# Another order of the attention work items in a fused attention and mixture-of-experts kernel on one core

## The reference

```python
q = _rope((x @ wq_w.T + wq_b).reshape(b, t, NH, HD).transpose(0, 2, 1, 3))
k = _rope((x @ wk_w.T + wk_b).reshape(b, t, NKV, HD).transpose(0, 2, 1, 3))
v = (x @ wv_w.T + wv_b).reshape(b, t, NKV, HD).transpose(0, 2, 1, 3)
k, v = jnp.repeat(k, G, axis=1), jnp.repeat(v, G, axis=1)
att = jnp.einsum('bhqd,bhkd->bhqk', q, k) / HD ** 0.5
att = softmax(where(causal, att, -inf))
y = jnp.einsum('bhqk,bhkd->bhqd', att, v)
x = layernorm(x + y.transpose(0, 2, 1, 3).reshape(b, t, c) @ cp_w.T + cp_b)
# then: x = layernorm(x + shared expert(x) + the four routed experts of each token(x))
```

## Time and profile before

| | |
|---|---|
| time, median of 3 runs | 551.11 us |
| span of the profiled execution | 548.3 us |
| PE busy | 525.8 us, 96% |
| DVE busy | 435.9 us, 79% |
| ACT busy | 372.3 us, 68% |
| POOL busy | 290.6 us, 53% |
| chain that ended last | PE 75%, DVE 10%, POOL 6% |
| granted TensorE clock, mean | 0.998 |

### The profile page before, as it was taken

One profiled execution on the slowest core, in us unless ns is written; L12 is line 12 of the kernel. 1 busy time (PEld: TensorE's weight loads), 2 busy tenths in 40 slices (PEclk: granted clock), 3 DMA queues, 4 the chain that ended last, 5 costly groups with the idle time before them and its releaser, 6 DMA issues.

```text
span 548.3 us, 12215 instructions
## 1 busy us (share of the span) xinstructions
PE 525.8 (96%) x3796; PEld 359.4 (66%) x3796; DVE 435.9 (79%) x1126; ACT 372.3 (68%) x841; POOL 290.6 (53%) x336
## 2 busy tenths in 40 slices
PE   8999999999999899989999898899999999999885
PEld 4656444444554454534433387799999999999874
DVE  2388989899889899999992177987878788787685
ACT  2444777787888688968879566366766667667534
POOL 5121232555412777267978856477644454545292
PEclk9999999999999999999999999999999999999999
DMA  5934174400523811321042352378544443341495
GB/s 150 179 66 65 31 191 145 82 8 21 91 62 88 207 58 46 82 81 51 32 128 82 104 178 66 112 227 262 159 139 128 130 118 111 111 133 46 160 414 194
DMA packets 53710, 64.96 MB, mean 118 GB/s; under 512 B 8091, under 2 KB 47406, under 8 KB 53648
## 3 DMA queue, kind: packets, MB, share of 16 engines
q1 hardware_dynamic: 45968, 46.45, 31.4%
q0 software_dynamic: 7056, 17.60, 9.2%
q10 hardware_dynamic: 624, 0.13, 0.1%
HBM read 32.49 MB, written 25.62 MB: 106 GB/s over the span
## 4 chain that ended last, share of the span: by engine, by line
PE 75%; DVE 10%; POOL 6%; issue 3%; ACT 2%; DMA 2%; SPq 1%; POOLq 0%; DVEq 0%; ACTq 0%
PE psH L1705 13%; PE psS L1506 12%; PE psO L1491 11%; PE psT L1476 10%; PE psS L1568 4%; PE psX L1673 3%; PE psG L1716 3%; PE psS L1511 2%; PE psS L1592 2%; POOL xs_scratch L766 2%; PE psY L1733 2%; PE psY L1730 2%; PE psY L1729 2%; PE psY L1732 2%; PE psY L1731 2%
## 5 line engine op out<-in xcount | busy, mean ns | idle before, releaser
L885 ACT ACTIVATE prob<-psT 128x512 f32<-128x512 f32 (+3 forms) x384 | 167.3, 495 | 51.6 <-PE psT L1476 49.0
L1161 DVE TENSOR_REDUCE MX<-psS 128x1 f32<-128x512 f32 (+3 forms) x344 | 182.6, 595 | 9.1 <-PE psS L1511 3.9
L1506 PE MATMUL psS<-KS,QS 96*128 96x512 bf16 (+3 forms) x384 | 109.9, 328 | 4.4 <-DVE MX L1161 2.5
L839 POOL DMA_INDIRECT y_scratch<-ys,dst x79 | 76.9, 973 | 65.7 <-ACT ys L1040 50.8
L1476 PE MATMUL psT<-QS,KS 98*128 98x512 bf16 (+3 forms) x384 | 107.0, 328 | 0.9 <-ACT prob L885 0.4
L795 POOL TENSOR_SCALAR_AFFINE_SELECT prob<-prob 128x512 f32<-128x512 f32 x64 | 42.4, 665 | 91.8 <-ACT prob L885 91.6
L1491 PE MATMUL psO<-prob,V 128*32 128x512 f32 (+3 forms) x768 | 81.3, 498 | 1.2 <-POOL prob L795 1.2
L1705 PE MATMUL psH<-wU,xh 128*128 (+1 forms) x380 | 80.8, 334 | 0.5 <-DVE z L1313 0.4
L766 POOL DMA_INDIRECT xs_scratch<-x1row,slotu x64 | 65.4, 1022 | 26.9 <-issue 16.2
L1476 PEld LDWEIGHTS psT<-QS,KS 98*128 98x128 bf16 x384 | 33.7, 97 | 52.9 <-ACT prob L885 34.6
L1506 PEld LDWEIGHTS psS<-KS,QS 96*128 96x128 bf16 x384 | 37.1, 98 | 45.4 <-DVE MX L1161 22.5
(11 more groups left out here) (260 smaller groups left out, 1003.0 us busy)
## 6 DMA issues: line engine op xcount, KB each, us to landing
xs<-xs_scratch SPq DMA_DIRECT2D x80, 134.0 KB
y<-y_scratch SPq DMA_DIRECT2D x16, 512.0 KB, 10.2
QS<-qp SPq DMA_DIRECT2D x48, 128.0 KB, 4.5
wU_raw<-in_L_ffn_w_routed_dram SPq DMA_DIRECT2D x32, 176.0 KB, 2.9
xs_scratch<-padrow SPq DMA_DIRECT2D x1, 2144.0 KB
xs_scratch<-padrow SPq DMA_DIRECT2D x16, 134.0 KB
x1row<-in_L_attn_x_dram SPq DMA_DIRECT2D x4, 512.0 KB, 5.8
out_dram<-x1row SPq DMA_DIRECT2D x7, 256.0 KB, 2.6
```

Source lines behind the costliest of these rows:

```text
L839: nc.gpsimd.indirect_dma_start(y4_dram, bass.IndirectOffsetOnAxis(ap=dst[:, n % NSEL, t:t + 1], axis=0), ys[:, n % NYS, t, :], None, bound ...
L885: nc.scalar.activation(prob[:, step % NPROB, h, 0:HALF - c0], ps[:, 0:HALF - c0], ACT.Exp).then_inc(s_Tfree, 1)
L1161: found = nc.vector.tensor_reduce(out=MX[:, c0 // HALF, heads[0]:heads[-1] + 1, i - TH * q], in_=src, op=ALU.max, axis=AX_X)
L1506: last = mm(ps[:, e * dist:e * dist + cols], QS[0:ROWS, QAT[(k // 2) % NSLOT], g % 2 * G + h, (i - TH * q) * P:(i - TH * q + 1) * P], KS[b ...
```

## The change

Only the string `ORDER` is different. Every stream has the same items in the same order; how the streams are interleaved is new nearly everywhere. The first of its nine lines:

```diff
 ORDER = """
-aaaaaaaadadpaaldppdlpdaaaapalaaaaapaapamalpppaxxaaaxxaaxaalxxxaaxxvamaxxavxxxaaaxavaxaxpaxmaxaxaaxxaaxvxaaaxxaexpavmaaxx
+aaaaaaaaddapalaldaaadaaaaaaaalpalampappaxaxaxaxaxaxaxaxxaxadxxdavmlvaaxavxxxaaaxaxaxaxvxaeaxxxavmxaxaxapaxxaaxaxxpavvvma
...
 """
```

More of the change, by code:

```diff
@@ L138 @@
 ORDER = """
-aaaaaaaadadpaaldppdlpdaaaapalaaaaapaapamalpppaxxaaaxxaaxaalxxxaaxxvamaxxavxxxaaaxavaxaxpaxmaxaxaaxxaaxvxaaaxxaexpavmaaxx
[L140 to L147, removed]
+aaaaaaaaddapalaldaaadaaaaaaaalpalampappaxaxaxaxaxaxaxaxxaxadxxdavmlvaaxavxxxaaaxaxaxaxvxaeaxxxavmxaxaxapaxxaaxaxxpavvvma
+axawxaaxaxaxenxlaaxaxvaxaaxaxaxvaxxawaxaxxwaxaxvvaxxaxeaaxaaxxavxdaaxxaxpxnamvvxnxapapaaxxaavaaeaxxanxxaaxvxraaxaxaxaaxd
+xsaaxawxvvxaxaarxaxaaxwaxxavxaxaaxaxvvmaaxaxxlraxxapxxaxaaxaraxavvaeaxaxaxaxaavvaxxaxaaxlaaxaxrxaxxaaxpxxarraavvvdmaxxna
+xxarxarapxaxxpxxxvvxxaaxaawxxaaxvaraxxeasaraxarxaaxvaxxadraaxavvarasxxaxaaxaxsaxxaxpxdaxmvvxxaaxaaraxxdaxvxaxxlaasxaxxvv
+rxaxwaawaxxaxeararxasxxvmvxalxxrxacxxacaxxsavvmaxaxxaaxaxacxaxaxvxxxaaaoxxlvxxaxnaxvvmaxcxeaxanxaxnaxxwxvvxccaaarxavxaxx
+aaarxaaxxavxcaaxexaaxraaxxrasrcxxavrcvaxxaarxaxcrxxxaaaaxvmrvxrxceaaaxaxxwcrwraxxxvxxoanrxxrvaxxaxcvvmaxaraxaarxwancsaxa
+xxeorxawxaarxcvsvxxxaaawxaxwoxxvvxexaxncxavwxaxxnxrwxacacsxxoaxvcvxaccracawlrxaxrxrcxaaaxaxvxaxcxrarxxmvsxaaarsraaxxvrvx
+aaxxaxwacxaaxvaearaxarsrxaacxssavaacrxxsaaxavarxarxcaarxaaxxcaraxaxcaaxaarxxvxaaxsaaxxvvmxaaxcxaxavaxcxxaarxxxwvxcaxxvca
+cexaxaxvcxcxxvxawxaxawxaxcaxaaxxcaxavsxaaxsxvxxonmxxxsvxxcxvxxcxxcvcxrcxxcnxxvwxexxxvxxxvxxcxvxxxvxxxvxxxcxxxxxvvvnsenc
 """
```

## The result

The changed kernel takes 546.05 us, the median of four executions (544.44 to 547.10), beside 553.49 us for four of the kernel before (550.45 to 556.66). The ratio is **0.9875, 95% interval 0.983 to 0.992**; the forecast was 545.8 us. A second measurement further down, with 12 executions, gave 548.84 us beside 552.55 and a ratio of 0.9934 (0.990 to 0.997). The forecast of 1.0% less lies between the two. The profiled execution has a span of 544.6 us, 3.7 less than before, and the whole difference is in the attention stage. Besides it I use a second profiled execution of the same kernel, called `after_again`.

What follows compares the result with a forecast made beforehand. VectorE was taken as the bound from group 10's first maximum to the last, TensorE before that. +2.0 - 6.3 - 1.0 = -5.3 on the 548.3 us span gives 543.0, plus 2.8 makes 545.8 us; range 541 to 552.

Steps and rivals of the forecast that it cites:

- The price of a visit: TensorE entering and leaving a stretch of weighted sums: 0.21 us each time, 34 fewer, 7.1 us less.
- A, before the cut: Attention stage up to group 10's first row maximum: +2.0 us (1 to 4), mainly +1.5 waiting for the query load.
- B: From group 10's first row maximum to the last maximum: -6.3 us, leaving 120.8 of 127.1.
- The disturbance of VectorE: Slowed `route`, `rank` and `wlow` instructions between group 10's first maximum and the last: -2.8 us (0 to -3.9).
- the +2.0: VectorE reaching group 10's first maximum late, with two maxima and a `rank` right ahead: +2.0 us (1 to 3.2).
- under 1.5: Sign: VectorE's waits for TensorE from group 10's first maximum to the last under 1.5 us; waits of 3.4 should go.
- the -2.6 for `route`, `rank` and `wlow`: After group 10's first maximum, VectorE has one `route` and one `rank` fewer, two `wlow` more: -2.6 us.
- VectorE decides: From group 10's first maximum to the last, VectorE stays the bound: 120.8 us against TensorE's 116.
- C: Behind the last maximum: earlier scatters give back a 1.2 us wait for masks; -1.0 us (-3 to +1).
- From the span to the median: Whole kernel: the median of the runs lies 2.8 us above the profiled span, so 543.0 becomes 545.8.
- TensorE's saving in full: Rival for the attention stage: VectorE loses all disturbance and is not late; 539.7 us, chance 0.16.
- The second rival: VectorE keeps what TensorE gives back: 2.8 us disturbance stays, tail gives nothing, start costs 3; 550.6 us, chance 0.26.
- The slow rival: Weighted sums in runs hold the `prob` buffers longer, delaying ScalarE: +13 us, 558.8 us, chance 0.10.

Runs made afterwards that it cites:

- before_runs: Kernel before with only weighted sums and `mrow` moved, into 71 stretches instead of 103; ratio 1.0166 to the kernel before.
- masks_first: `scat_later` with further scatters and the first subtraction for wU also moved behind masks on GpSimd; ratio 0.9868 to the kernel before.
- proj_early: Changed kernel with one query projection moved back ahead of the first row maximum; ratio 0.9945 to the kernel before.
- rank_early: Changed kernel with the second quarter's `rank` three maxima of group 13 earlier; ratio 0.9936 to the kernel before.
- scat_later: Changed kernel with five scatters of the second quarter moved behind group 12's last four diagonal scores; ratio 0.9931 to the kernel before.

## Why the prediction was right, and where it was not

**The price of a visit** (0.21 us from two pairs of neighbours) holds: the same steps, read all over the traces, are 0.09 us to enter and 0.12 to leave, and 40 visits more made the stage 7.4 us longer. That is above the 0.166 us which the prediction took from the Trainium skill (TensorE: Matmul & The Clock Gate, Single matmul latency) as an estimate.

**A, before the cut** (+2.0): +1.7, with the first maximum and the wait for the load where they were put. That 3.9 us of visits cancel against work done earlier is confirmed: TensorE's own work from the first maximum to the cut grew by 3.9 us, of which 3.6 are the two projections that now stand behind the first maximum.

**B** (-6.3): -5.9 in `after_again` and -4.2 in the profiled execution. The size was right, but by errors that offset, which is luck. The disturbance of VectorE fell by 3.3 us (5.6 to 2.3, each instruction but the maxima against the fastest of its kind), a little more than the 2.8 put down; one weight subtraction meets the third `route`, as the sum had it. The lock that the prediction named from the Trainium skill (SBUF — State Buffer, Who interferes with whom) agrees with that pair in `after_again`: GpSimd's subtraction from 265.01 to 266.68, VectorE's L1117 1.27 us long from 265.49. The masks could have kept the 2.8 by the same rule and did not: beside that pair only one instruction of this part lost more than 0.2 us in `after_again`, L1106 at 263.66 with 0.46, during a scatter and the mask behind it. VectorE comes to group 10 3.0 us behind TensorE, not 0.7, which is +2.3 for the +2.0. But its waits fell from 3.4 to 2.2 us, not to nothing, and were 3.8 in the profiled execution: "under 1.5" was wrong. With the -2.6 for `route`, `rank` and `wlow` as forecast that makes -4.8; some 1.1 us of the gain stands in none of my terms.

**"VectorE decides"** is the step of the account that failed. Its signs were VectorE's waits for TensorE under 1.5 us and TensorE's waits for maxima grown; the first were 2.2 and 3.8 us, and the second fell from 2.3 to 1.2. By the prediction's own words part B is wrong if VectorE waits for TensorE there. TensorE's own work in B fell by 6.6 us, and with VectorE relieved the two orders are as far apart as ever. Two engines were the bound together, and the order relieved both. Read alone, 119.4 busy of 127.1 us suggested one.

**C** (-1.0): -1.2; the masks' wait at the end went from 1.2 to 0.4 us.

**From the span to the median** I added 2.8 us. In every execution the time lies 1.8 above the span (546.37 and 544.6 in the profiled one); the rest was the clock's falls in others. The changed kernel has more of them: in the second measurement its median lies 5.7 us above the profiled span of 543.1, at a median granted clock of 0.993 beside 0.996 for before. So 2.8 was too little there, and that the first median came out at 546.05 is partly luck.

**The rivals.** TensorE's saving in full: its own work did fall by 7.2 us, and 1.9 us of waits took the difference. The second rival is out: the disturbance of VectorE went, the tail gave 1.2 us and the start cost 1.7. The slow rival put its price (+13) on buffers held by weighted sums. In the changed kernel exponentials waited 0.5 us at most for a weighted sum. In `before_runs` the danger was real, at 10 us, but by another path: ScalarE shows no wait for a weighted sum's buffer there; it is starved of scores and then flooded.

**What was missing** is the wait of 1.6 us at 238 and the clock behind it. I looked at VectorE and at the exponentials for the new waits. That GpSimd runs in order, that a scatter in its queue waits for `rank`, and that masks stand behind it, was in the prediction only for the end of the stage (its part C), where I had it as a gain. The second quarter's `rank` had moved from among group 14's maxima into group 13's, and with it its first scatters from behind group 12's masks to ahead of them. `masks_first` puts that at 1.9 us, without the clock.

## What to carry over

A saving on a full engine can be lost elsewhere: moving work together can starve the neighbour, so one has to look at the engine that is fed. When two engines are both above 90% in a stage, neither need be "the" bound; relieving one shows how far the other stands behind it. In a queue in order, an item that waits for a late result (a scatter for its slot numbers) carries its wait to whatever stands behind it.

## What the runs showed of the hardware

A wait of TensorE can cost about twice its length. In the changed kernel the granted clock was 0.58 and 0.56 in the two stretches of 2 us behind the wait of 1.64 us at 240 us, mostly the lower of the two levels, 1.2 GHz, and this fall cost 1.6 us more. The granted clock was 0.50 to 0.65 in the same way behind waits of 1.41 us at 34 us in `proj_early`, 2.18 at 222 in `rank_early` and 2.78 at 247 in `before_runs`, the last for a maximum.

A wait of this length doesn't settle it. The changed kernel has the wait of 1.6 us at the same instruction in `after_again` and keeps 1.00; the kernel before waits 1.72 us for a maximum at 241 us and keeps 1.00. In `scat_later` and `masks_first` the clock fell at 29 us, some 5 us behind the wait of 1.3 us for the query load, and `after_again`, with the same waits up to there, kept 1.00. What decides between the two stays open.

Over the 12 executions of the changed kernel in the second measurement the span went from 543.1 us at a mean clock of 1.000 to 549.9 at 0.990. This is why a median of this kernel lies microseconds above its best profile. Its gain over before was 1.25% in one measurement, where its four executions had mean clocks of 0.996 to 0.999, and 0.66% in the other, where the median was 0.993.
